# Sorting whole token rows by expert in memory, and turning routed tiles with VectorE block transposes in place of TensorE transposes

## The reference

```python
scores = jax.nn.softmax(x @ gate_w.T, axis=-1)
topk_w, topk_ids = lax.top_k(scores, 6)              # 6 of 16 experts
topk_w = topk_w / (topk_w.sum(-1, keepdims=True) + 1e-20)
combine = jnp.einsum('tk,tke->te', topk_w, one_hot(topk_ids, 16))
def body(acc, ew):                                   # over 16 experts
    w13_e, w2_e, c_e = ew                            # (704, 512), (512, 352)
    return acc + c_e[:, None] * swiglu(x, w13_e, w2_e), None
out = out + swiglu(x, sw13, sw2)                     # shared expert, width 704
x = x + tanh(g_ffn) * out
```

## Time and profile before

| | |
|---|---|
| timed runs | median 1436.95 us of 3 (1435.53 to 1438.42) |
| profiled execution, first to last instruction | 1435.5 us |
| TensorE matmuls busy | 1349.9 us (94%) |
| VectorE, ScalarE, GpSimd busy | 787.5, 730.9, 949.3 us |
| granted TensorE clock, mean | 0.976 of full speed; 1.00 in stage B |
| shared tiles | about 490 to 705 us |
| routed tiles | about 705 to 1430 us |

### The profile page before, as it was taken

How to read it: one execution, slowest core, us unless ns; L and a number is a source line. 1 busy time by engine, 2 the same in 40 slices (tenths; PEclk the granted TensorE clock), 3 DMA queues, 4 the chain that set the end, 5 groups by cost and what they waited for, 6 DMA issues and landing times.

```text
span 1435.5 us, 32257 instructions
## 1 busy us (share of the span) xinstructions
PE 1349.9 (94%) x8480; PEld 1210.6 (84%) x8481; DVE 787.5 (55%) x1364; ACT 730.9 (51%) x1317; POOL 949.3 (66%) x671
## 2 busy tenths in 40 slices
PE   6897998997898899999999999999999999999996
PEld 2686887887888799999998989989889988899885
DVE  6878898898989854653333333333333333333331
ACT  5898897898889464343332333323333333332321
POOL 0588898898988747887456665566645666546632
PEclk8899999999999999999999999999999999999999
DMA  4120122222242365645455435555445544454432
GB/s 137 38 74 31 53 67 96 67 73 91 75 146 72 133 129 106 142 84 141 83 141 145 131 63 144 139 147 137 104 94 137 141 135 104 95 147 131 76 68 36
DMA packets 65042, 149.13 MB, mean 104 GB/s; under 512 B 16976, under 2 KB 17616, under 8 KB 62656
## 3 DMA queue, kind: packets, MB, share of 16 engines
q0 software_dynamic: 31024, 62.10, 22.9%
q1 hardware_dynamic: 33392, 81.21, 17.5%
q10 hardware_dynamic: 560, 4.98, 1.0%
HBM read 101.50 MB, written 48.99 MB: 105 GB/s over the span
## 4 chain that ended last, share of the span: by engine, by line
PE 65%; DVE 3%; issue 1%; POOL 0%; ACT 0%; DVEq 0%; POOLq 0%; ACTq 0%
PE bank L1719 19%; PE bank L1699 19%; PE bank L1700 18%; PE bank L1687 3%; PE bank L1710 3%; DVE hs L1172 1%; PE bank L1604 1%; PE bank L1590 1%; PE bank L1602 0%; POOL hc L949 0%; DVE sc L1226 0%; PE bank L1665 0%; DVEq L1375 0%; DVE xl L1363 0%; DVE du L1186 0%
## 5 line engine op out<-in xcount | busy, mean ns | idle before, releaser
L949 POOL TENSOR_TENSOR hc<-hs,crow 128x512 f32<-128x512 f32 x254 | 322.6, 1302 | 91.8 <-DVE hs L1172 84.6
L1699 PE MATMUL bank<-w,xh 128*128 (+1 forms) x1088 | 368.7, 340 | 7.6 <-issue 4.2
L1015 POOL DMA_INDIRECT out_x<-ys,aid x104 | 171.2, 1646 | 275.0 <-issue 215.7
L1700 PE MATMUL bank<-w,xh 128*128 (+1 forms) x1088 | 351.2, 323 | 0.0
L1172 DVE TENSOR_TENSOR_SCAN hs<-dA,bank 128x512 f32<-128x512 f32 x256 | 295.8, 1208 | 47.9 <-PE bank L1604 32.0
L1719 PE MATMUL bank<-w,ah 128*128 (+1 forms) x816 | 264.7, 405 | 2.7 <-DVE al L1399 2.7
L1399 DVE TENSOR_TENSOR al<-bank,ah 128x384 fp32r<-128x384 f32 x136 | 75.8, 557 | 331.0 <-ACT ah L862 283.2
L1699 PEld LDWEIGHTS bank<-w,xh 128*128 128x128 f32 x1088 | 204.3, 188 | 35.9 <-issue 32.1
L1700 PEld LDWEIGHTS bank<-w,xh 128*128 128x128 f32 x1088 | 206.4, 190 | 2.3
L868 ACT COPY ys<-bank 128x512 f32<-128x512 f32 x136 | 79.9, 587 | 195.9 <-PE bank L1719 191.5
L1700 PE MATMUL bank<-w,xl 128*128 (+1 forms) x544 | 175.9, 323 | 0.0
(11 more groups left out here) (184 smaller groups left out, 2051.7 us busy)
## 6 DMA issues: line engine op xcount, KB each, us to landing
wraw<-in_wall SPq DMA_DIRECT2D x16, 2176.0 KB
crow<-c_rows SPq DMA_DIRECT2D x64, 256.0 KB, 3.3
xt<-token_rows_turned SPq DMA_DIRECT2D x32, 256.0 KB
out_x<-ys POOLq DMA_DIRECT2D x32, 256.0 KB
wraw<-in_wall ACTq DMA_DIRECT2D x2, 2176.0 KB
token_rows<-rowb SPq DMA_DIRECT2D x4, 1028.0 KB
xrow<-in_x SPq DMA_DIRECT2D x4, 1024.0 KB, 7.0
out_x<-xrow SPq DMA_DIRECT2D x4, 1024.0 KB, 4.9
```

The source lines that it names most:

```text
L949: nc.gpsimd.tensor_tensor(hc[:, j, :], hs[:, j, :], crow[:, n % 4, :], ALU.mult).then_inc(hc_done, 1)
L1015: pool.indirect_dma_start(out_rows, bass.IndirectOffsetOnAxis(ap=aid[:, s:s + 1], axis=0), ys[:, s, :], None, bounds_check=TOKENS - 1, oob ...
L1699: nc.tensor.matmul(gate_bank[:, 0:I], xx, columns(w, off + ww + k * 2 * I, I), start=first, stop=last)
L1700: mm = nc.tensor.matmul(up_bank[:, 0:I], xx, columns(w, off + ww + k * 2 * I + I, I), start=first, stop=last)
```

## The change

Whole rows are sorted, instead of a list of ids. During shared tiles 2 to 29 GpSimd issues 112 indirect DMAs (`scatter`, four to a tile), each of which writes 128 rows of 532 floats from an SBUF copy of a batch (`srow`, loaded by SP with `batch_rows`) to the place of the row's expert in `expert_rows`; 16 of them write zero rows behind each expert's last token. The token's id is stored in the row as a number. A routed tile is then 128 neighbouring rows of that buffer. SP loads it with five plain DMAs (`expert_load`): four take a quarter of the features each to 32 partitions, as pieces of 128 floats, and one takes the columns behind the features (`tail`). VectorE transposes it in 32x32 blocks in one instruction (`spread`) from `xs` to `xq`. The features then lie on the partitions in another order than before, so the routed experts' weights are loaded in that order too (`expert_set`, four DMAs of quarter rows and one for the down weights). `turn_x`, `gather`, `list_tokens` and the copies of `gid` go. `wraw` has two buffers, and ScalarE issues the loads of the routed experts' weights, at each change of expert behind its copy (`fetch_behind`). The gate keeps the id in a spare column, and the table has two more steps.

```diff
-AHEAD = 5
-FIRST_ROWS = {NS - 3: (NS, NS + 1), NS - 2: (NS + 2,), NS - 1: (NS + 3, NS + 4)}
+TAIL = ROW - H
+IDCOL = TAIL - 2
+REGION = (TT + 1) * P
+PADS = E * REGION
+SEG = H // 4
+SCATTERS = TOPK * TT + E
+SCATTERS_AT = dict.fromkeys(range(2, 30), 4)
+PARTS = 5
...
-               8: [("exp", 3)], TT - 3: [("fetch", 2)]}
+               8: [("exp", 3)], TT - 3: [("fetch", 2)], NS - 6: [("fetch", 3)]}
...
-    list_d = nc.dram_tensor("token_lists", (P * NR, 1), I32, kind="Internal").ap()
+    rows_d = nc.dram_tensor("token_rows", (TOKENS, ROW), F32, kind="Internal").ap()
+    sorted_d = nc.dram_tensor("expert_rows", (PADS + P, ROW), F32, kind="Internal").ap()
...
-        xt = alloc(ctx, "xt", [P, 4, ROW])
+        xt = alloc(ctx, "xt", [P, 4, H])
...
+        wraw = alloc(ctx, "wraw", [P, 2 * WCOLS])
...
+        srow = (srow0, alloc(ctx, "srow1", [P, TC, ROW]))
+        xs = alloc(ctx, "xs", [P, 4, TC, SEG])
+        xq = alloc(ctx, "xq", [P, 2, HK, P])
+        tail = alloc(ctx, "tail", [P, 4, TAIL])
...
+            def batch_rows(b):
+                if b == 0:
+                    sp.wait_ge(wl_done, 1)
+                if b == 1:
+                    sp.wait_ge(turned_stored, 16 * NB)
+                    sp.wait_ge(base_stored, 16 * NB)
+                sp.wait_ge(rows_stored, 16 * (b + 1))
+                sp.wait_ge(wts_stored, 16 * (b + 1))
+                if b > 1:
+                    sp.wait_ge(listed[b - 2], 16 * TOPK * TC)
+                sp.dma_start(srow[b % 2][:], rows_v[b]).then_inc(srow_in[b % 2], 16)
+            def expert_load(t, s):
+                if not (isinstance(t, int) and t < NS + 4):
+                    apart(sp, spread_done, t - NS - 3, "sp")
+                    apart(sp, aid_done, t - 3, "sp")
+                first = sp.value_load(meta[0:1, 4, bass.ds(t, 1)], min_val=0, max_val=PADS)
+                own = sorted_d[bass.ds(first, P), :]
+                for a in range(4):
+                    sp.dma_start(xs[32 * a:32 * a + 32, s, :, :], own[:, a * SEG:(a + 1) * SEG].rearrange("(c j) v -> j c v", c=TC)).then_inc(expert_in[s], 16)
+                sp.dma_start(tail[:, s, :], own[:, H:ROW]).then_inc(expert_in[s], 16)
...
+            batch_rows(1)
+            for t in range(12, 15):
                 x_load(t)
             weights(NB - 1, 0)
-            for t in range(20, NS):
+            x_load(15)
+            batch_rows(2)
+            for t in range(16, 21):
                 x_load(t)
-            with sp.Fori(3, NX) as e:
-                fetch(e)
+            batch_rows(3)
+            for t in range(21, 24):
+                x_load(t)
+            sp.wait_ge(pads_ready, 1)
+            sp.dma_start(sorted_d[PADS:PADS + P, :], padrow[:]).then_inc(pad_stored, 16)
+            for t in range(24, NS):
+                x_load(t)
             sp.wait_ge(meta_ready, 2)
+            sp.wait_ge(pad_stored, 16)
+            for b in range(NB):
+                sp.wait_ge(listed[b], 16 * TOPK * TC)
+            sp.wait_ge(pads_listed, 16 * E)
+            groups = routed_groups(sp)
+            for k in range(4):
+                expert_load(NS + k, k)
+            with sp.Fori(0, groups - 1) as i:
+                for k in range(4):
+                    expert_load(4 * i + NS + 4 + k, k)
...
-                act.wait_ge(wl_done, e)
-                act.dma_start(wraw[:], wall[bass.ds(e, 1)].rearrange("a p c -> p (a c)")).then_inc(raw_in, 16)
+                if e == 1:
+                    act.wait_ge(summed, NB * DS * J)
+                else:
+                    act.wait_ge(wl_done, e - 1)
+                if e == 1:
+                    shared_set(act, e, wraw[:, raw_at(e):raw_at(e) + WCOLS])
+                else:
+                    expert_set(e, raw_at(e))
+            def expert_set(e, at):
+                own = wall[bass.ds(e, 1)].rearrange("a p c -> (a p) c")
+                for a in range(4):
+                    act.dma_start(wraw[32 * a:32 * a + 32, bass.ds(at, W2AT)].rearrange("i (b n) -> i b n", b=HK),
+                                  own[:, a * 2 * I:(a + 1) * 2 * I].rearrange("(b i) n -> i b n", b=HK)).then_inc(raw_in, 16)
+                act.dma_start(wraw[:, bass.ds(at + W2AT, WCOLS - W2AT)], own[:, W2AT:WCOLS]).then_inc(raw_in, 16)
+            def fetch_behind(e, t):
+                behind = act.value_load(meta[0:1, 5, bass.ds(t, 1)], min_val=0, max_val=NX - 1)
+                apart(act, wl_done, e, "act")
+                expert_set(behind, raw_at(e + 1))
...
-                    act.wait_ge(xt_turned, t + 1)
-                    source = banks[4][:]
+                    act.wait_ge(spread_done, t - NS + 1)
+                    source = xq[:, s, :, :].rearrange("p k m -> p (k m)")
...
+                    fetch_behind(e, t)
...
-            fetch(1)
             x_high(0, 0)
             x_high(1, 1)
+            fetch(1)
...
-            def gather(t, s):
-                if isinstance(t, int) and t < NS + 4:
-                    pool.wait_ge(xl_done, t - 3)
-                else:
-                    apart(pool, xt_turned, t - 3, "pool")
-                    apart(pool, cc_done, t - 3, "pool")
-                apart(pool, gid_done, t + 1, "pool")
-                pool.indirect_dma_start(xt[:, s, :], None, rows_d[:, :],
-                                        bass.IndirectOffsetOnAxis(ap=gid[:, s:s + 1], axis=0)).then_inc(gathered[s], 16)
...
-            def list_tokens(i):
-                if i == 0:
-                    pool.wait_ge(blank_in, 16)
-                    pool.wait_ge(plan_in, 16 * N_PLAN)
-                if i % TOPK == 0:
-                    pool.wait_ge(pos_ready, i // TOPK + 1)
-                for c in range(4 * i, 4 * i + 4):
-                    chunk = c // (TC * TOPK) * TC + c % TC
-                    pool.indirect_dma_start(list_d[:, :], bass.IndirectOffsetOnAxis(ap=posi[:, c:c + 1], axis=0),
-                                            ids[:, chunk:chunk + 1], None).then_inc(listed, 16)
+            def scatter(i):
+                if i < TOPK * TT:
+                    b = i // (TOPK * TC)
+                    if i % (TOPK * TC) == 0:
+                        pool.wait_ge(srow_in[b % 2], 16 * (b // 2 + 1))
+                        pool.wait_ge(pos_ready, b + 1)
+                    pool.indirect_dma_start(sorted_d[:, :], bass.IndirectOffsetOnAxis(ap=posi[:, i:i + 1], axis=0),
+                                            srow[b % 2][:, i % TC, :], None).then_inc(listed[b], 16)
+                else:
+                    e = i - TOPK * TT
+                    if e == 0:
+                        pool.wait_ge(pads_ready, 1)
+                    pool.indirect_dma_start(sorted_d[:, :], bass.IndirectOffsetOnAxis(ap=padi[:, e:e + 1], axis=0),
+                                            padrow[:], None).then_inc(pads_listed, 16)
...
-                    pool.wait_ge(wts_stored, 16 * NB)
-                    pool.wait_ge(rows_stored, 16 * (NB + 1))
-                for late in FIRST_ROWS.get(t, ()):
-                    gather(late, late % 4)
...
-                if 0 <= t - LISTS_LATE < TT * TOPK // 4:
-                    list_tokens(t - LISTS_LATE)
-                elif t - LISTS_LATE == TT * TOPK // 4:
-                    pool.wait_ge(listed, 16 * TOPK * TT)
-                    pool.dma_start(lists[:], list_d.rearrange("(p t) a -> p (t a)", p=P)).then_inc(ids_in, 16)
+                for i in range(scattered, scattered + SCATTERS_AT.get(t, 0)):
+                    scatter(i)
+                scattered += SCATTERS_AT.get(t, 0)
+            assert scattered == SCATTERS
...
-            with pool.Fori(0, groups - 2) as i:
+            with pool.Fori(0, groups) as i:
...
+                chained(nc.vector.tensor_copy(wts[:, :, E:E + 1].rearrange("p c a -> p (c a)"), ids[:, b * TC:(b + 1) * TC]))
...
-                chained(nc.vector.scalar_tensor_tensor(out=column[:], in0=slot[:], scalar=float(TT), in1=begin[:], op0=ALU.mult, op1=ALU.add))
-                chained(nc.vector.tensor_scalar(meta[:, 4, :], column[:], float(-NS), 0.0, ALU.add, ALU.max))
+                chained(nc.vector.scalar_tensor_tensor(out=column[:], in0=slot[:], scalar=float(TT + 1), in1=begin[:], op0=ALU.mult, op1=ALU.add))
+                chained(nc.vector.tensor_scalar(column[:], column[:], float(-NS), float(P), ALU.add, ALU.mult))
+                chained(nc.vector.tensor_scalar(beyond[:], tileno[:, 0, :], end_e[:, E - 1:E], float(2 * PADS), ALU.is_ge, ALU.mult))
+                chained(nc.vector.tensor_tensor(column[:], column[:], beyond[:], ALU.max))
+                chained(nc.vector.tensor_scalar(meta[:, 4, :], column[:], 0.0, float(PADS), ALU.max, ALU.min))
...
+            def spread(t, s4, m=None):
+                if isinstance(t, int) and t < NS:
+                    return
                 rows_in(dve, t, s4, m, "dve")
-                at_least(dve, am_done, t - 1)
```

(26 more changed lines are left out.)

148 lines of the change are left out of this document (77 added, 71 removed).

## The result

The change makes the kernel slower by 9%: 1564.93 us median of 4 runs (1563.49 to 1567.72) against 1437.68 of 4 (1435.53 to 1441.47) for the kernel before on the same chip. The ratio is 1.0884, 95% interval 1.0863 to 1.0905. The prediction was 1429, range 1403 to 1452, faster at 0.62; the time lies 113 us above the range. The cause was on none of its lists.

A forecast was written before the change was run, and what follows sets the result against it. The prediction took TensorE's own work to bound the routed loop. Against the profiled span of 1435.5, -45.8 + 14 + 23.5 + 0.5 = -7.8 gave span 1427.7, time about 1429, range 1403 to 1452.

The forecast's parts named there:

- What replaces them on VectorE: Routed tiles, VectorE: one 128x512 block transpose a tile, 0.7 us, hidden in idle time; earlier high and low parts counted none.
- The transposes go, -45.8: Routed tiles, TensorE: four transposes of 0.44 us a tile leave the chain in 104 tiles, 45.8 us less.
- The block transpose at 0.7 us, hidden: Head of VectorE's routed tile: 0.7 us, hidden behind 2.89 us idle, up to about 2.9 us.
- Its other estimate, 1.24: VectorE's block transpose from the skill page: four 128x128 at 311 ns, 1.24 us, the sum unmoved.
- The expert changes, +14: Fifteen changes: ScalarE's five DMA issues delay ah, a hole of 1.55 us ahead of down; 14 us more, ends 0 and 28.
- today's changes: Changes of expert in the kernel before: about 0.6 us each, taken off the 1.55 us hole.
- The scatters: Shared tiles, GpSimd: 112 row scatters at 0.98 us issue, last at 701.4; DMA engines 173 to 213 of 184 us.
- the range of 0.60 to 0.96: DMA engines, shared tiles: us for each row scatter, taken from gathers; 67 to 107 us for 112.
- The turn, +23.5: Shared to routed tiles: loads wait for all scatters, down of tile 30 at 720.6, not 697.1; 23.5 us, ends 14.5 and 43.
- The rivals: Other outcomes: small give-backs 1400 to 1406 (0.26), full DMA engines 1448 to 1470 (0.17), scatter at 1.59 us 1490 (0.05), late loads (0.07).
- Late loads: Routed loop: quarter loads to 32 partitions at half rate come late, transposes' time not saved; 1445 to 1475, chance 0.07.

The follow-up runs named there:

- experiment 1: Changed kernel, but the block transpose writes to PSUM banks and `x_high` and `x_low` of routed tiles read there: 1469.95 us, ratio 1.0218.
- experiment 3: Kernel before, but `x_low` of routed tiles reads the untransposed gathered row in SBUF, and a gather also waits for it: 1589.19 us, ratio 1.1057.
- experiment 10: Kernel of experiment 8 with only the block transpose's output put back into SBUF: 1533.11 us, ratio 1.0661.
- experiment 5: Kernel of experiment 1, with the weights' five DMAs at a change of expert issued by SyncE instead of ScalarE: 1442.14 us, ratio 1.0037.
- experiment 8: Kernel of experiment 5 plus zero rows written by SyncE and TensorE's table reads moved ahead, also over the loop's edge: 1385.50 us, ratio 0.9638.

## Why the prediction was wrong

**The step that failed** is one sentence under "What replaces them on VectorE": "The high and low parts of x are now ready before the up projection instead of just at its start, which can only help". The block transpose was priced, 0.7 us, and the readers of its output were not. `x_low` changed its source from a PSUM bank to SBUF, and with that met a pass of GpSimd of 9.4 us, 15 times. The diff has it in one line (`source = xq` in `x_low`, shown under experiment 1), and the trace of before had both sides: GpSimd's weight pass, and the subtraction that ran beside it at 0.69 us from PSUM. These are such a pass and the subtraction in it, in the kernel before:

```profile
801.51 9.57 POOL L987 TENSOR_TENSOR w<-wraw,w 128x4352 f32 x1
...
801.98 0.69 DVE L1363 TENSOR_TENSOR xl<-bank,xh 128x512 fp32r<-128x512 f32 x1
```

The subtraction with both inputs in SBUF (L1363 from `xt`) also took 0.69 us, but only in the shared tiles, where no such pass ran. That row hid the price. Experiments 1, 3 and 10 show it from three sides: 95, 151 and 148 us.

The Trainium skill has the rule, SBUF — State Buffer, "SBUF: two separate sides": VectorE and GpSimd share a pair of ports, and a VectorE operation with two inputs in SBUF and a GpSimd operation that reads SBUF shut each other out, whichever is first, for its whole instruction. The runs agree: 6.80, 8.40 and 9.29 us for a subtraction of 0.69, and 2.37 where GpSimd's pass was cut in four, with GpSimd's next piece 0.4 us longer. On which of the two goes first they are less clear: at one change of experiment 3 the profile has the subtraction start at 1149.97 and the pass at 1150.25, and still the subtraction ended last, after 10.22 us. The prediction drew on another section of that page and not on this one.

**The transposes go, -45.8.** Half right. The work left TensorE, but plain tiles fell by 0.20 us, not by 0.44. The prediction took the shared tile's 6.29 for a routed one; a routed tile also has table reads in TensorE's queue, and in the kernel before the transposes stood ahead of the down projection and covered most of their time. Without them 76 us of "issue" stood ahead of the up projection's first line in experiment 5 (matmuls and weight loads counted together), and 8 in experiment 8. With the reads moved in both kernels a plain tile is 6.26 against 6.74, which is the 0.44 and a little more.

**The block transpose at 0.7 us, hidden.** Right: 0.71. Its other estimate, 1.24, is 1.75 times what was measured.

**The expert changes, +14.** Right mechanism, size low: the hole was 1.87 us on average (1.58 to 2.20), not 1.55, and the tile of the change took 8.70 instead of 7.9 us, 12 us more in all. The issues took what the earlier trace rows gave, 1.94 us for four and 0.37 for the last, but the first began 0.99 us behind the copy's start, where 0.35 was taken, and `ah` came 1.97 us behind the copy's end, where the prediction had 1.0. The 0.6 us that it took off for "today's changes" did not stand in this tile: before, it took 6.89 us against 6.82 for the others. They stood in the tile behind, 7.42, and did not go away. A lower granted clock behind the hole, which the prediction did not count, came at three of the 15. Whether SyncE's and ACT's issues wait for one another was not tried by itself.

**The scatters.** Right: 0.96 us each (0.98 predicted), the last issued at 698.4 (701.4). On the DMA engines, by queue from 518 to 702:

```profile
q0 software_dynamic: 12924, 37.72, 69.7%
q1 hardware_dynamic: 7152, 11.75, 21.1%
q10 hardware_dynamic: 1440, 4.46, 7.5%
```

The adds of before took 50.5 us (58.5 of q0, less 8 for lists and gathers), and the DMA view of that stretch counts 29 of them, 1.74 us each. The view of after counts 27 adds and 111 scatters: 128.2 us of q0 less 47 are 0.73 us for each scatter, in the range of 0.60 to 0.96. The lower end of that range rested on a slip: with 1.74 or 1.75 us an add, and not 1.9, the same sum gives 0.76 for a gather, so that 0.73 lies in the range by luck. Together the three took 181 us of 184: full, with hardly a backlog.

**The turn, +23.5.** Right mechanism, too large: down(30) came 11.4 us later and the next interval was 2.3 longer, 13.7. The first load was issued at 703.25, 4.8 us behind the last scatter, where 11.5 were taken:

```profile
703.25 2.16 SPq L683 DMA_DIRECT2D xs<-expert_rows  x4
...
707.45 0.71 DVE L1461 STREAM_TRANSPOSE xq<-xs 128x512 f32<-128x512 f32 x1 [18.44 <-DMA tail<-expert_rows]
...
708.74 1.22 PE L1792 MATMUL bank<-w,ah 128*128 x2 [13.87 <-DVE al L1483]
```

**The rivals.** Late loads did not come: in the loop nothing waits for one. Their condition was half there. In the routed stretch the loads of weights took 16.3% of 833 us for 15 sets, 9.1 us each against 12.5% of 707 for 14 sets, 6.3 us, in whole rows; the loads of rows took 16.1%, 1.3 us a tile, against 0.6 to 0.8 for a gather. The DMA share was 0.56, so it cost nothing. The Trainium skill's rule (SBUF — State Buffer, "Door 1: The DMA port swizzle") gives up to double for such loads; these are 1.4 times for a set, of which a third of the bytes goes to all partitions as before.

Summed against the prediction's span of 1427.7, of which the measured one is 134.3 off: 106 us for the tiles behind a change (6.64 more instead of 0.44 less, 15 times), 20 for the tiles of a change (1.81 more instead of 0.51), 17 for the plain tiles, -10 for the turn, 133 in all.
